# Gated experts in a four-layer decoder: bias sum on GpSimd, gate weights later, scores of head pairs on 64-row halves

## The reference, cut to what matters

```python
def _L2_ffn_ref(x, ...):
    h = jax.nn.relu(xf @ dp_w1 + dp_b1)
    entropy = jax.nn.softplus(h @ dp_w2 + dp_b2)[:, 0]
    norm = jnp.clip((entropy - TH_LO) / (TH_HI - TH_LO), 0.0, 1.0)
    k_tok = jnp.clip(jnp.round(MIN_E + norm * (E - MIN_E)).astype(jnp.int32), MIN_E, E)
    top_logits, top_idx = jax.lax.top_k(xf @ gate_w + gate_b, E)
    masked = jnp.where(jnp.arange(E)[None, :] < k_tok[:, None], top_logits, -jnp.inf)
    dense_w = zeros((T, E)).at[..., top_idx].set(jax.nn.softmax(masked, axis=-1))
    hid = jax.nn.relu(jnp.einsum('td,edh->teh', xf, ew1) + eb1[None, :, :])
    y = jnp.einsum('teh,ehd->ted', hid, ew2) + eb2[None, :, :]
    return jnp.einsum('te,ted->td', dense_w, y)
def _L3_xattn_ref(...):          # H, DH, K_TOP = 4, 32, 32; 120 keys
    scores = jnp.einsum('bthd,bghd->bhtg', Q, K) / sqrt(DH)     # masked keys: -inf
    topv, topi = jax.lax.top_k(scores, K_TOP)
    attn = zeros_like(scores).at[..., topi].set(jax.nn.softmax(topv, axis=-1))
    c_t = jnp.einsum('btg,bgd->btd', attn.mean(axis=1), V) * text_mask
    scale_in, shift_in = jnp.split(c_t @ W_film_in + b_film_in, 2, axis=-1)
    x = layernorm(x_text) * (1.0 + mod_gate * scale_in) + mod_gate * shift_in
```

## Time and profile before

| | us |
|---|---|
| median of 3 timed runs (4915.15 to 4919.07) | 4916.27 |
| the profiled execution | 4864.6 |
| its span, first to last instruction | 4862.9 |
| PE busy in the span | 4467.8 (92%) |
| DVE busy | 3197.9 (66%) |
| ACT busy | 2002.1 (41%) |
| POOL busy | 1819.2 (37%) |
| mean granted TensorE clock | 0.966 |

### The profile page before, as it was taken

One profiled execution on the slowest core, in us unless ns is written; L12 is line 12 of the kernel. 1 busy time (PEld: TensorE's weight loads), 2 busy tenths in 40 slices (PEclk: granted clock), 3 DMA queues, 4 the chain that ended last, 5 costly groups with the idle time before them and its releaser, 6 DMA issues. The chain is left out here.

```text
span 4862.9 us, 90653 instructions
## 1 busy us (share of the span) xinstructions
PE 4467.8 (92%) x31852; PEld 3475.8 (71%) x31852; DVE 3197.9 (66%) x9752; ACT 2002.1 (41%) x4152; POOL 1819.2 (37%) x2248
## 2 busy tenths in 40 slices
PE   7999869999995999799996999999999977999999
PEld 5666547778884888667764788888888734777866
DVE  5888779987553332178883788888888853444444
ACT  3555447764442232145552333433443332222234
POOL 2222136542553332155440233333333313655632
PEclk9999979999997999899998999999999989999999
DMA  4666512245223222222222011110110064222233
GB/s 112 154 155 156 123 60 72 73 130 169 60 58 66 71 72 68 57 70 69 76 60 75 26 33 31 28 29 28 29 30 26 23 217 143 87 93 86 89 112 105
DMA packets 332893, 391.33 MB, mean 80 GB/s; under 512 B 66485, under 2 KB 301466, under 8 KB 321690
## 3 DMA queue, kind: packets, MB, share of 16 engines
q1 hardware_dynamic: 319130, 360.28, 26.2%
q0 software_dynamic: 13312, 25.25, 2.2%
HBM read 296.33 MB, written 89.10 MB: 79 GB/s over the span
## 5 line engine op out<-in xcount | busy, mean ns | idle before, releaser
L2693 PE MATMUL fa_h<-fa_xnT,fa_w 128*128 128x256 f32 x2048 | 484.8, 382 | 0.0
L2705 PE MATMUL fa_y<-fa_w,fa_hT 128*128 128x256 f32 x2048 | 462.5, 379 | 0.0
L2693 PEld LDWEIGHTS fa_h<-fa_xnT,fa_w 128*128 128x128 f32 x2048 | 379.8, 190 | 82.1 <-issue 27.5
L2568 ACT ACTIVATE fa_hT<-fa_h,fa_b 128x256 f32<-128x256 f32 x512 | 214.6, 469 | 533.8 <-PE fa_h L2693 472.4
L2705 PEld LDWEIGHTS fa_y<-fa_w,fa_hT 128*128 128x128 f32 x2048 | 386.5, 190 | 65.3 <-issue 15.4
L516 DVE TENSOR_REDUCE a_mx<-a_score 128x16 f32<-128x1920 f32 x128 | 276.0, 2156 | 55.7 <-PE a_score L700 55.6
L3085 ACT ACTIVATE m_hT<-m_h,m_b 128x256 f32<-128x256 f32 x256 | 107.3, 470 | 365.0 <-PE m_h L3148 365.0
L1700 PE MATMUL r_h<-r_xnT,r_rw 128*128 128x256 f32 x1024 | 246.9, 389 | 0.0
L2007 ACT ACTIVATE e_hT<-e_h,e_b 128x256 f32<-128x256 f32 x256 | 107.3, 470 | 335.4 <-PE e_h L2061 335.4
L1846 POOL DMA_INDIRECT e_xg<-moe_rows,e_idx x64 | 128.6, 2009 | 307.7 <-issue 254.5
L3148 PE MATMUL m_h<-m_hnT,m_w 128*128 128x256 f32 x1024 | 235.7, 379 | 2.5 <-ACT m_hnT L3075 2.5
(11 more groups left out here) (463 smaller groups left out, 10826.9 us busy)
## 6 DMA issues: line engine op xcount, KB each, us to landing
a_floor<-a_lowest SPq DMA_DIRECT2D x64, 960.0 KB, 8.5
cv_toep<-kernels SPq DMA_DIRECT2D x16, 2048.0 KB, 9.7
x<-a_xo SPq DMA_DIRECT2D x96, 256.0 KB, 4.3
f_xb<-x SPq DMA_DIRECT2D x64, 256.0 KB, 3.5
f_xres<-x SPq DMA_DIRECT2D x64, 256.0 KB, 3.0
a_xb<-x SPq DMA_DIRECT2D x64, 256.0 KB, 3.1
e_w<-in_L_ffn_ew SPq DMA_DIRECT2D x16, 1024.0 KB, 7.2
a_cb<-in_ctx SPq DMA_DIRECT2D x96, 90.0 KB, 3.1
```

The lines of the kernel that those rows point to most:

```text
L2568: act.activation(hT[e % 2][:, 2 * m + c, :], h_ps[j % 2][:, c, :], ACT.Relu, bias=b1[:, f:f + 1]).then_inc(h_ready, 1)
L2693: last = pe.matmul(h_ps[j % 2][:, c, :], w1[:, e, k, f:f + P], xnT[it.p][:, k, :], start=k == 0, stop=k == KD - 1)
L2705: last = pe.matmul(bank[:, t * D:(t + 1) * D], hT[e % 2][:, k, t * P:(t + 1) * P], w2[:, e, k, :], start=k == 0, stop=k == KE - 1)
```

## The change

The sum of the bias rows leaves PE. `turn_weights`, `wT_out` and `bias` are gone, and so is DVE's `begin_sum`. b2 is now broadcast to all 128 partitions (128x1024 elements instead of 4x256). POOL's new `begin_sum(e)` multiplies the bias row of expert e with the tokens' gate weight into xo (e = 0) or into a tile biased, which a second instruction adds to xo; `add_residual` adds the residual. Steps 0 and 1 stand at the end of POOL's slot (lag 4), steps 2, 3 and the residual behind the key mask (lag 5). `weigh_gates` stands behind `norm_stats` on DVE instead of ahead of `sum_heads(0)`. Experts' results now take the banks y_ps in turn, e % 2, and `down(e)` waits for one sum less. Film values on PE stand behind `up(6)`.

For the scores kd has 2 x 120 columns instead of 4 x 120: rows 0 to 63 hold the keys of heads 0 and 1, rows 64 to 127 those of heads 2 and 3. Each tile t takes two products on 64 rows, one on either half, into two banks of a tile ba (the old a_ps and b_ps); `take_scores` reads them in four parts of 240, and waits for all four products.

The diff without its smaller places (other counts of the same semaphores, names of banks):

```diff
     w1, w2, b1 = st.sb("w1", [P, NG, KD, HE]), st.sb("w2", [P, NG, KE, D]), st.sb("b1", [P, NG * KE])
-    b2 = st.sb("b2", [NG, D])
+    b2, biased = st.sb("b2", [P, NG, D]), st.sb("biased", [P, TL, D])
     gw, gb = st.sb("gw", [P, KD, NG]), st.sb("gb", [P, NG])
...
 
-    t_ps, g_ps, a_ps, b_ps = (st.ps(n, [P, 512]) for n in ("t", "g", "a", "b"))
+    t_ps, g_ps = (st.ps(n, [P, 512]) for n in ("t", "g"))
+    ba_ps = st.ps("ba", [P, 2, 512])
+    b_ps, a_ps = ba_ps[:, 0, :], ba_ps[:, 1, :]
+    pair = st.sb("pair", [P, 2])
     h_ps = [st.ps(f"h{p}", [P, 2, S]) for p in two]
...
         def _(sp):
-            for a, n in ((gw, "gate_w"), (dw1, "dp_w1"), (db1, "dp_b1"), (dw2, "dp_w2"), (b1, "eb1"), (b2, "eb2")):
+            for a, n in ((gw, "gate_w"), (dw1, "dp_w1"), (db1, "dp_b1"), (dw2, "dp_w2"), (b1, "eb1")):
                 sp.dma_start(a[:], w[n]).then_inc(small, 16)
+            sp.dma_start(b2[:].rearrange("p e d -> p (e d)"), w["eb2"].rearrange("e d -> (e d)").partition_broadcast(P)).then_inc(small, 16)
             sp.dma_start(gb[:], w["gate_b"].partition_broadcast(P)).then_inc(small, 16)
...
                 pool.memset(lg[p][:], -3e38).then_inc(padded, 1)
+            pool.tensor_tensor(pair[:], const["heads4"][:, 0:2], const["heads4"][:, 2:4], ALU.add).then_inc(padded, 1)
+            pool.wait_ge(padded, 3)
 
...
                 inverse_root(pool, Chain(pool, roots, it.i, 2), mv[it.p][:, :, 1], rs[it.p][:], const)
+
+            def begin_sum(e):
+                def step(it):
+                    p = it.p
+                    c = Chain(pool, weighed, it.i, BIAS)
+                    c.n = max(0, 2 * e - 1)
+                    if e == 0:
+                        pool.wait_ge(gate, GATE * (it.i + 1))
+                        if it.reused():
+                            pool.wait_ge(stored[p], 16 * it.h)
+                            pool.wait_ge(xn3_ready, it.i - 1)
+                    if e or it.reused(1):
+                        c.wait()
+                    out = biased if e else xo[p]
+                    c.add(pool.tensor_tensor(out[:], b2[:, e:e + 1, :].to_broadcast([P, TL, D]),
+                                             wgt[p][:, :, e].unsqueeze(2).to_broadcast([P, TL, D]), ALU.mult))
+                    if e:
+                        c.wait()
+                        c.add(pool.tensor_tensor(xo[p][:], xo[p][:], biased[:], ALU.add))
+                return step
+
+            def add_residual(it):
+                p = it.p
+                pool.wait_ge(weighed, BIAS * (it.i + 1))
+                pool.wait_ge(r_in[p], 16 * (it.h + 1))
+                pool.tensor_tensor(xo[p][:], xo[p][:], xres[p][:], ALU.add).then_inc(begun, 1)
 
...
                 if it.reused(1):
-                    pool.wait_ge(s_done, 2 * it.i)
-                pool.tensor_tensor(kd[:], kT[:].unsqueeze(1).to_broadcast([P, NH, SK]),
-                                   const["heads4"][:].unsqueeze(2).to_broadcast([P, NH, SK]), ALU.mult).then_inc(kd_ready, 1)
+                    pool.wait_ge(s_done, it.i)
+                pool.tensor_tensor(kd[:], kT[:].unsqueeze(1).to_broadcast([P, 2, SK]),
+                                   pair[:].unsqueeze(2).to_broadcast([P, 2, SK]), ALU.mult).then_inc(kd_ready, 1)
 
...
             pipeline(pool, B, DEPTH, [
-                (6, roots_of_sum), (6, roots_of_normed), (6, key_mask), (6, affine), (6, spread_k), (7, scale_heads(0)), (7, scale_heads(1)),
-                (6, negate_max(0)), (6, negate_max(1)), (1, roots_of), (7, mix(0)), (7, mix(1))])
+                (6, roots_of_sum), (6, roots_of_normed), (6, key_mask), (5, begin_sum(2)), (5, begin_sum(3)), (5, add_residual), (6, affine),
+                (6, spread_k), (7, scale_heads(0)), (7, scale_heads(1)), (6, negate_max(0)), (6, negate_max(1)), (1, roots_of), (7, mix(0)), (7, mix(1)),
+                (4, begin_sum(0)), (4, begin_sum(1))])
 
...
 
-            def wT_out(it):
-                dve.wait_ge(w_turned, it.i + 1)
-                if it.reused(1):
-                    dve.wait_ge(b_done, it.i)
-                dve.tensor_copy(wT[:], g_ps[0:NG, 0:S]).then_inc(wT_ready, 1)
-
-            def begin_sum(it):
-                p = it.p
-                dve.wait_ge(b_done, it.i + 1)
-                dve.wait_ge(r_in[p], 16 * (it.h + 1))
-                if it.reused():
-                    dve.wait_ge(stored[p], 16 * it.h)
-                    dve.wait_ge(xn3_ready, it.i - 1)
-                dve.tensor_tensor(xo[p][:], y_ps[p][:].rearrange("p (t d) -> p t d", t=TL), xres[p][:], ALU.add).then_inc(summed, 1)
-
             def add_expert(e):
...
                     p = it.p
-                    dve.wait_ge(summed, SUM * it.i + e + 1)
+                    if e == 0:
+                        dve.wait_ge(begun, it.i + 1)
+                    else:
+                        dve.wait_ge(summed, SUM * it.i + e)
                     dve.wait_ge(y_done, NG * it.i + e + 1)
                     for t in range(TL):
-                        last = dve.scalar_tensor_tensor(xo[p][:, t, :], y_ps[(1 + p + e) % 2][:, t * D:(t + 1) * D], wgt[p][:, t, e:e + 1],
+                        last = dve.scalar_tensor_tensor(xo[p][:, t, :], y_ps[e % 2][:, t * D:(t + 1) * D], wgt[p][:, t, e:e + 1],
                                                         xo[p][:, t, :], ALU.mult, ALU.add)
...
                 c = Chain(dve, pick, it.i, PICK)
-                for t, bank in ((0, b_ps), (1, a_ps)):
-                    dve.wait_ge(s_done, 2 * it.i + t + 1)
+                dve.wait_ge(s_done, it.i + 1)
+                for t in range(TL):
                     if it.reused(1):
                         dve.wait_ge(kept_exp, 2 * it.i + t - 1)
-                    c.add(dve.scalar_tensor_tensor(sc[t][:], bank[:, 0:NH * SK].rearrange("p (h k) -> p h k", k=SK), (P // NH) ** -0.5,
-                                                   kmf[it.p][:].unsqueeze(1).to_broadcast([P, NH, SK]), ALU.mult, ALU.add))
+                    for half in two:
+                        last = dve.scalar_tensor_tensor(sc[t][:, 2 * half:2 * half + 2, :],
+                                                        ba_ps[:, half, t * 2 * SK:(t + 1) * 2 * SK].rearrange("p (h k) -> p h k", k=SK), (P // NH) ** -0.5,
+                                                        kmf[it.p][:].unsqueeze(1).to_broadcast([P, 2, SK]), ALU.mult, ALU.add)
+                    c.add(last)
 
...
              pipeline(dve, B, DEPTH, [
-                (6, sum_stats), (7, pick_round(2)), (6, norm_sum), (4, rank_gates), (5, begin_sum), (7, pick_round(3)), (7, keep_taken),
-                (7, weigh_heads(0)), (7, weigh_heads(1)), (4, weigh_gates), (7, sum_heads(0)), (7, sum_heads(1)), (5, add_expert(0)), (6, take_scores), (6, pick_round(0)),
-                (5, add_expert(1)), (4, wT_out), (1, norm_stats), (7, film_out(0)), (6, pick_round(1)), (2, norm), (5, add_expert(2)),
+                (6, sum_stats), (7, pick_round(2)), (6, norm_sum), (4, rank_gates), (7, pick_round(3)), (7, keep_taken),
+                (7, weigh_heads(0)), (7, weigh_heads(1)), (7, sum_heads(0)), (7, sum_heads(1)), (5, add_expert(0)), (6, take_scores), (6, pick_round(0)),
+                (5, add_expert(1)), (1, norm_stats), (4, weigh_gates), (7, film_out(0)), (6, pick_round(1)), (2, norm), (5, add_expert(2)),
                 (7, film_out(1)), (5, add_expert(3))])
...
                 last.then_inc(g_done, 1)
-
-            def turn_weights(it):
-                pe.wait_ge(gate, GATE * (it.i + 1))
-                for t in range(TL):
-                    last = pe.transpose(g_ps[0:NG, t * P:(t + 1) * P], wgt[it.p][:, t, :], const["ident"][:])
-                last.then_inc(w_turned, 1)
-
-            def bias(it):
-                pe.wait_ge(wT_ready, it.i + 1)
-                if it.reused(1):
-                    pe.wait_ge(summed, SUM * it.i - 1)
-                for t in range(TL):
-                    last = pe.matmul(y_ps[it.p][:, t * D:(t + 1) * D], wT[:, t * P:(t + 1) * P], b2[:], start=True, stop=True)
-                last.then_inc(b_done, 1)
 
...
                     pe.wait_ge(h_ready, KE * (NG * it.i + e + 1))
-                    if e or it.reused(1):
-                        pe.wait_ge(summed, SUM * it.i + e)
-                    bank = y_ps[(1 + it.p + e) % 2]
+                    if e >= 2 or it.reused(1):
+                        pe.wait_ge(summed, SUM * it.i + e - 1)
+                    bank = y_ps[e % 2]
                     for t in range(TL):
...
                     pe.wait_ge(film_ready, 2 * it.i - 2)
-                for t, bank in ((0, b_ps), (1, a_ps)):
-                    pe.matmul(bank[:, 0:NH * SK], qT[:, t * P:(t + 1) * P], kd[:].rearrange("p h k -> p (h k)"),
-                              start=True, stop=True).then_inc(s_done, 1)
+                for t in range(TL):
+                    for half in two:
+                        rows = slice(half * P // 2, (half + 1) * P // 2)
```

(11 more changed lines are left out.)

20 lines of the change are left out of this document (10 added, 10 removed).

## The result

The changed kernel takes 4864.11 us (median of 4 runs, 4862.53 to 4866.02), the kernel before 4915.71 (4906.95 to 4919.07): a ratio of 0.9902, with a 95% interval of 0.9891 to 0.9914, so 42 to 54 us less. Forecast were 4875 us and 41 us less, with a range from 4853 to 4908.

The account below looks back on a forecast made before the run. A POOL and DVE loop of 37.6 us, above PE's 36.89, was taken to set the period. Gains of 28 and 11 in the iterations, 1 at the start and 1 in the drain made -41 us: 4875 us, range 4853 to 4908.

Parts of the forecast that it names:

- What PE needs: PE's passes per iteration fall from 38.77 to 36.89 us: bias product 1.25, transposed gate weights 0.22, scores 0.41 saved.
- The pieces of POOL: POOL's new steps: bias products 1.04 us each, sums 1.27, key spreading 0.59 instead of 0.99; busy time 13.2 to 22.0.
- dear products: Rival: POOL's products cost 1.27 and each take_scores part 0.1 more; loop 38.7 us, time 4901, up to 4912; chance 0.15.
- products at 2.24: Slower rival: POOL's broadcast products cost 2.24 us each; loop 42.4, time 4990; chance 0.11.
- The loop: POOL from mix 1 to scale_heads 0 (19.67 us) plus DVE from sum_heads 0 to film_out 1 (17.94): 37.6 us.
- Who binds: POOL and DVE together set the period at 37.6 us, above PE's 36.89; forecast chance 0.50.
- The rival of PE as the bound: PE stays the bound because the loop is 0.7 us shorter than added up: 58 us gained, 4858; chance 0.20.
- Waits at the scores and the film values: PE waits about 0.7 us an iteration at its scores or film values, ended by POOL's fa_kd or DVE's fa_sc.
- The iterations' sum: 24 full-loop slots gain 28 us; six slots at start and end, where PE binds, gain 11.
- Start and end of the stage: Start: 14.29 us wait for gate weights shrinks to 2.3 gained against 1.8 for b2's load, net 1; drain gains 1.
- Carrying the difference over to the median: The 41 us gain from the profiled 4864.6 us is applied unchanged to the timed median 4916.27, giving 4875.

Follow-up runs that it names:

- the kernel with the affine step moved: Changed kernel with POOL's affine step moved from ahead of spread_k to behind scale_heads 1: 4802.82 us on the second chip, 4845.18 us on the third.
- the run with the rows loaded later: Kernel with affine behind scale_heads 1, plus b2's broadcast load issued after the experts' weights: 4845.63 us.
- the scores alone: Kernel before with only the scores changed (keys on two halves, eight passes of 240 columns, film values behind up(6)), bias left on PE: 4853.73 us, ratio 0.9977.
- the bias alone: Changed kernel with the scores, spread_k and take_scores of the kernel before: 4830.32 us, ratio 0.9923 to the kernel before.
- the chip of the first group: Changed kernel with, in turn: begin_sum 0 and 1 before mix 1, 4852.22 us; one more POOL step, 4904.71; weigh_gates back, 4884.47; film_values back, 4872.49.
- the sums between the mixes: Changed kernel with begin_sum 0 and 1 moved in POOL's slot from behind mix 1 to between mix 0 and mix 1: 4852.22 us, ratio 0.9888.

## Why the prediction was right, step by step

- **What PE needs**: forecast 36.89, measured 36.89, in the iterations ahead of the full loop and in all of the kernel with the affine step moved. The scores save 0.40 by themselves.
- **The pieces of POOL**: the products at 1.04 (forecast 1.04, rival 1.27 or 2.24), sums 1.27, `spread_k` 0.59. The rivals of dear products and of products at 2.24 are out. (The one step of 2.3 us is a sum, beside `keep_taken`.)
- **The loop**: forecast 37.6, measured 37.72. DVE's part from sum_heads 0 to film_out 1 was put at 17.88 and takes 17.87; mix 1 with its hand-over 1.71, as forecast. From there to the mean over the heads the forecast had 18.02 with the last hand-over, and it is 18.14. 0.08 of the difference is the block by `keep_taken`: put at 0.97 on the affine step, it is 1.05 on a sum, and 0.71 where it is shared.
- **Who binds**: POOL and DVE, not PE. Taking 3.5 or 2.6 us out of the loop makes the period PE's; adding 1.23 to it adds 1.20. The rival of PE as the bound (4858) lay nearer to the measured time than the forecast did, but by chance: it needs iterations of 36.9, and they took 37.7.
- **Waits at the scores and the film values**: the two places named; the usual iteration is 0.83 us longer than what PE needs (forecast 0.7).
- **The iterations' sum**: forecast 28 + 11 = 39 us, measured 39.0. That this agrees to the tenth is in part luck: 25 iterations are the loop's, not 24, and each gains 1.13 in the mean instead of 1.17.
- **Start and end of the stage**: this is the term that was mis-sized. The start was put at 2.8 us gained and 1.8 lost to the load of b2. The loss is right (1.9; the load made 1.7 of it, by the run with the rows loaded later), but the gain is 7.5: where PE waited 14.29 us for the first gate weights, it now waits 6.66 for the norm behind the next load of x and 2.36 for the copy, 5.3 less, and the stretch no longer holds the bias product and the turned weights. The drain, put at 1 gained, lost 0.9.
- **Carrying the difference over to the median**: I took the traces' gain as that of the timed runs. 43.7 us in the traces, 51.6 and 51.1 in the timed runs of two chips; the intervals reach down to 42 and 44. On the third chip the profiled execution of the kernel before took 4907.2, 7 us less than the median of the runs beside it, and those of the changed kernel did not (4866.0 against 4864.1, 4868.1 against 4863.5). By the third chip's own traces the stage and the gap give 43.2 us for the changed kernel and 63.3 with the affine step moved, the times 51.1 and 69.4: 6 to 8 us more both times. No trace shows a timed run of before, so where these are stays open. On the other two chips traces (stage and gap) and times agree within about 2 us: 12.2 and 12.8 for the scores alone, 35.0 and 36.2 for the bias alone, 65.7 and 63.7 with the affine step moved; and on the chip of the first group 56.0 and 58.0, 7.3 and 5.5, 26.5 and 25.7, 39.3 and 37.7, in the order of its runs.

## What to carry to other kernels

Look for the loop when work moves to an engine with idle time: POOL was idle 15 of 38 us, and yet each microsecond put between two hand-overs of the loop cost one. Ask of each step who needs its result and when; the one whose reader is furthest away (here affine, for mix 0) goes into the wait that is left, and that gave 20 us more in the stage without an instruction less. And compare stages, not spans, when profiles come from different chips.

## What the runs showed of the hardware

- A DVE tensor_scalar with one SBUF tensor as input (L227, 128x256) goes from 0.41 us to 1.20 in the median when POOL's 128x512 steps stand beside it; a cast of 8 elements (L2407) from 0.17 in the median of the changed kernel to 1.13, with 1.24 at most, in the one with the sums between the mixes. Reductions were not touched (`fa_mean` as above, and L2527 with 0.64 in both).
- The block does not come out the same each time: the same two steps of DVE cost POOL 1.05 us in most iterations and 0.71 in others, which makes iterations of 37.72 and of 37.35.
- The kernel before on the third chip had its router stage end 22 us later than on the second, spread over its batches (0.9 us each in most), and the attention stage took 22 more on top. In the router stage ScalarE's copy r_lT starts 1.3 us, in the median, after the end of the product that it reads, instead of 0.07, and the trace names no reason for the delay (it puts waits there down to that product or to "remote"). What the chips do differently there was not tested.
